# A state-space block's schedule: convolution one unit earlier, token products at the end of a job, inverse deviation left in PSUM, hinted loop edge

## The reference

```python
def _mamba_block(x, in_w, conv_w, conv_b, A_log, xd_w, xB_w, xC_w, dtp_w, dtp_b, D, out_w, g, b):
    xn = _layer_norm(x, g, b)
    xs, z = jnp.split(xn @ in_w, 2, axis=-1)
    xc = silu(causal_depthwise_conv4(xs) + conv_b)
    delta = softplus(xc @ xd_w @ dtp_w + dtp_b)
    Bm, Cm = xc @ xB_w, xc @ xC_w
    dA = exp(delta[..., None] * A)
    dBx = (delta * xc)[..., None] * Bm[:, :, None, :]
    y = _ssm_scan(dA, dBx, Cm) + D * xc       # h = dA * h + dBx; y = sum over 16 states of h * C
    return y * silu(z) @ out_w + x
fwd = blk(blk(x, 0), 1)
bwd = blk(blk(x[:, ::-1], 2), 3)[:, ::-1]
return jnp.concatenate([fwd, bwd], axis=-1) @ merge_w
```

## Time and profile before

| | |
|---|---|
| median of 3 runs | 10373.58 us (10369.56 to 10376.43) |
| the profiled execution's own time | 10389.18 us |
| its span, first to last instruction | 10387.4 us |
| busy, share of the span | PE 80%, PEld 66%, DVE 78%, POOL 68%, ACT 57% |
| Mamba phase, first scan to last | 144.1 to 8662.4 us |
| granted TensorE clock, mean over the span | 0.87 |

### The profile page before, as it was taken

How to read it: one execution, slowest core, us unless ns; L and a number is a source line. 1 busy time by engine, 2 the same in 40 slices (tenths; PEclk the granted TensorE clock), 3 DMA queues, 4 the chain that set the end, 5 groups by cost and what they waited for, 6 DMA issues and landing times. The chain is left out here.

```text
span 10387.4 us, 152898 instructions
## 1 busy us (share of the span) xinstructions
PE 8344.1 (80%) x42776; PEld 6881.5 (66%) x42776; DVE 8087.7 (78%) x10482; ACT 5899.2 (57%) x9202; POOL 7059.5 (68%) x7227
## 2 busy tenths in 40 slices
PE   5877777777878787878787877787877776999998
PEld 4666666666666666666666666676666664777776
DVE  4888889888988888888898888888888894333332
ACT  4565656565665666566566666665566662444443
POOL 4888888888888888888888888888888883000000
PEclk8888888888888888888888888888888887999998
DMA  2222222222222222222222222222222220000000
GB/s 93 94 89 99 92 98 91 99 92 93 92 94 93 90 98 93 90 79 90 89 98 93 98 91 97 93 98 92 90 93 96 92 90 25 11 10 10 12 9 9
DMA packets 414916, 819.68 MB, mean 79 GB/s; under 512 B 148919, under 2 KB 194139, under 8 KB 414043
## 3 DMA queue, kind: packets, MB, share of 16 engines
q1 hardware_dynamic: 410328, 806.69, 22.3%
q10 hardware_dynamic: 3714, 2.89, 0.1%
HBM read 783.16 MB, written 26.30 MB: 78 GB/s over the span
## 5 line engine op out<-in xcount | busy, mean ns | idle before, releaser
L776 ACT ACTIVATE decay<-delta,neg_a 128x512 f32<-128x512 f32 x4096 | 2793.0, 688 | 2484.5 <-DVE h_ps L978 1112.7
L544 POOL TENSOR_TENSOR bu<-b_all,u_buf 128x512 f32<-128x512 f32 x3072 | 3579.4, 1191 | 151.6 <-DVE h_ps L978 148.3
L978 DVE TENSOR_TENSOR_SCAN h_ps<-decay,bu 128x512 f32<-128x512 f32 x2304 | 2782.6, 1222 | 454.6 <-ACT decay L776 376.3
L1233 PE MATMUL y_ps<-ident,ch 128*128 128x128 f32 x16384 | 2579.9, 309 | 637.4 <-DVE ch L998 362.7
L1233 PEld LDWEIGHTS y_ps<-ident,ch 128*128 128x128 f32 x16384 | 2226.7, 161 | 1016.2 <-DVE ch L998 484.4
L556 POOL TENSOR_TENSOR ch<-ch,c_all 128x512 f32<-128x512 f32 x1024 | 1325.5, 1294 | 1112.1 <-DVE ch L978 910.0
L998 DVE TENSOR_TENSOR ch<-h_ps,c_all 128x512 f32<-128x512 f32 x3072 | 1977.2, 671 | 0.0
L547 POOL TENSOR_TENSOR bu<-b_all,u_buf 128x514 f32<-128x514 f32 x1024 | 1245.6, 1237 | 66.8 <-issue 56.3
L1117 PE MATMUL w_ps<-xn,in_w 128*128 128x257 f32 x4096 | 1074.8, 408 | 170.5 <-ACT xn L665 83.6
L982 DVE TENSOR_TENSOR_SCAN h_ps<-decay,bu 128x256 f32<-128x256 f32 x1536 | 1046.7, 737 | 125.3 <-POOL bu L547 98.2
L1117 PEld LDWEIGHTS w_ps<-xn,in_w 128*128 128x128 f32 x4096 | 799.9, 206 | 320.2 <-issue 81.1
(11 more groups left out here) (258 smaller groups left out, 11583.9 us busy)
## 6 DMA issues: line engine op xcount, KB each, us to landing
b_all<-bc_dram SPq DMA_DIRECT2D x512, 514.0 KB, 8.6
c_all<-bc_dram SPq DMA_DIRECT2D x512, 514.0 KB, 10.0
in_w<-in_L_attn_in_w SPq DMA_DIRECT2D x64, 1024.0 KB, 5.0
diag_store<-diag_dram SPq DMA_DIRECT2D x256, 256.0 KB, 2.9
x_in<-in_x SPq DMA_DIRECT2D x128, 256.0 KB, 2.6
out_w<-in_L_attn_out_w SPq DMA_DIRECT2D x64, 512.0 KB, 3.9
skip_diag<-skip_dram SPq DMA_DIRECT2D x64, 256.0 KB, 4.1
h_mid<-h_cur SPq DMA_DIRECT2D x32, 257.0 KB, 2.2
```

Of the source, the lines that this page charges most:

```text
L544: pool.tensor_tensor(bu[:, s % NBU, 0:NB * L].rearrange("p (b t) -> p b t", b=NB), b_all[:, n // NU, n % NU, :, 1:], u_buf[:, c % 2, :, 1: ...
L776: func(decay[:, s % NDP, :].rearrange("p (b t) -> p b t", b=NB), delta[:, c, :, 1:S], ACT.Exp, scale=neg_a[:, k, c, n:n + 1]).then_inc(dec ...
L978: dve.tensor_tensor_scan(h, decay[:, s % NDP, :], bu[:, s % NBU, 0:NB * L], 0.0, ALU.mult, ALU.add).then_inc(scan_done, 1)
L1233: last = pe.matmul(y_ps[:, k, :], ch[:, s % NPR, k * P:(k + 1) * P], ident[:, :], is_transpose=True, start=False, stop=(n == NST - 1 and k ...
```

## The change

It moves rows of the hand-written schedule and changes one buffer:

- `CONV_AT` is 14 in place of 15: projection, convolution, Silu, `xp` and the early step sizes of the next job stand one unit earlier (the Silu in unit 23). `y_at` keeps 12 or 14 and 18 and has 26 in place of 25; as its list position moves too, `y1` stands behind both halves of convolution 1.
- ACT copies the third chunk's sums in unit 25, behind the Silu, in place of just ahead of it in unit 24.
- The token products of job 2 move from units 10 to 13 to units 26 to 29, ACT's copies of them from units 12 and 14 to 28 and 30. The first two `x_in` loads go ahead of everything in job 2; the other six stand in `bring_bc`, two behind each of the pairs 1, 2 and 3 of `b_all` and `c_all`.
- The inverse deviation of a job is computed in place in PSUM (ACT's Ln and Exp), and DVE's two multiplications of the layer norm read it there; `rstd` in SBUF is left to the tokens and the step sizes. In jobs 1 to 3 DVE normalizes within unit 13, not behind it, and ACT applies gain and bias in unit 13, not 14. In job 4 `norm_at` is 10 in place of 11.
- The loop is opened with `hint_back_edge=True`: a row BRANCH_PREFETCH_HINT at the head of every round, on every engine.

```diff
@@ -25,7 +25,7 @@
 BLOCK_OF_JOB = (0, 2, 1, 3)
-CONV_AT = 15
+CONV_AT = 14
 EPS = 1e-5
@@ -49,8 +49,7 @@
-        first = norm[:2] + ["t0"] + norm[2:] + ["t1"] if tokens else norm
-        steps = first + conv + ["xp", "dt0", "dt1", "dt2", "dt3"]
+        steps = norm + conv + ["xp", "dt0", "dt1"] + (["t0", "t1"] if tokens else []) + ["dt2", "dt3"]
         return [(name, 4 if name in ("t0", "t1") else jj) for name in steps]
@@ -66,10 +65,8 @@
-        for name, before in [("y2", "xp"), ("y1", "cv1")] + [("y0", "t1"), ("y0", "xs0")]:
+        for name, before in [("y2", "dt1"), ("y1", "xs2"), ("y0", "xs0")]:
             at = [i for i, key in enumerate(keys) if key[0] == before]
-            if name == "y0" and ((name, jj) in keys or before == "t1" and not at):
-                continue
             keys = keys[:at[0]] + [(name, jj)] + keys[at[0]:] if at else [(name, jj)] + keys
@@ -102,14 +99,14 @@
     def y_at(jj):
-        return (14 if jj == 4 else 12), CONV_AT + 3, CONV_AT + 10
+        return (14 if jj == 4 else 12), 18, 26
...
     def norm_at(jj):
-        return 11 if jj == 4 else 9
+        return 10 if jj == 4 else 9
@@ -314,7 +311,7 @@
             period(0, 0, True, False)
-            with eng.Fori(0, GROUPS - 1) as g:
+            with nc.Fori(0, GROUPS - 1, engines=[eng.engine], hint_back_edge=True) as g:
                 for jj in (1, 2, 3, 4):
@@ -388,10 +385,12 @@
                                      ).then_inc(bc_loaded[n], 16)
-
-            def load_x(g, jj):
-
-                for n in range(8):
+                    if jj == 3 and not is_final(g) and n in (1, 2, 3):
+                        load_x(g, 4, (2 * n, 2 * n + 1))
+
+            def load_x(g, jj, part=range(8)):
+
+                for n in part:
                     c, b, half = n // 4, n // 2 % 2, n % 2
@@ -433,6 +432,8 @@
+                if jj == 2 and not is_final(g):
+                    load_x(g, 4, range(2))
                 if not first:
@@ -443,8 +444,6 @@
                     load_weights(jj + 1)
-                    if jj == 2 and not is_final(g):
-                        load_x(g, 4)
                     load_skip(g, jj + 1)
@@ -653,6 +652,12 @@
                 w = banks(name, g, jj)
+                if kind == "job":
+
+                    func(w[:, :, 0:S], w[:, :, 0:S], ACT.Ln, bias=eps_t[:, 0:1]).then_inc(rstd_logs, 1)
+                    act.wait_ge(rstd_logs, job_count(g, jj, 1, 1))
+                    func(w[:, :, 0:S], w[:, :, 0:S], ACT.Exp, scale=-0.5).then_inc(rstd_ready, 1)
+                    return
                 func(rstd[:, :, :], w[:, :, 0:S], ACT.Ln, bias=eps_t[:, 0:1]).then_inc(read_of(name, g, jj), 1)
@@ -660,7 +665,7 @@
                 k = BLOCK_OF_JOB[jj % 4]
-                act.wait_ge(xhat_ready, job_count(g, jj, 1, 1))
+                act.wait_ge(read_of("var", g, jj), nth("var", g, jj))
                 for c in range(CM):
@@ -846,11 +851,11 @@
                     centred(g, jj + 1, 1)
-                if jj == 2 and not is_final(g) and u == 12:
-                    tokens(g, 4, 0)
+                if jj == 2 and not is_final(g) and u in (28, 30):
+                    tokens(g, 4, (u - 28) // 2)
                 if u == norm_at(jj) + 3:
                     inverse_deviation("job", g, jj + 1)
-                if u == norm_at(jj) + (4 if jj == 4 else 5):
+                if jj == 4 and u == norm_at(jj) + 4:
                     gain_and_bias(g, jj + 1)
@@ -885,8 +890,8 @@
                     centred(g, jj + 1, 0)
-                if jj == 2 and not is_final(g) and u == 14:
-                    tokens(g, 4, 1)
+                if jj != 4 and u == norm_at(jj) + 4:
+                    gain_and_bias(g, jj + 1)
                 if u == CONV_AT + 1:
@@ -908,12 +913,10 @@
                     lead(g, jj, NU * u + NDP, last)
-                    if u % PAIRS == 1 and u // PAIRS != 3 and not (first and u == 1):
+                    if u % PAIRS == 1 and not (first and u == 1):
                         token_rows(g, jj - (u == 1), (u // PAIRS - 1) % CI)
...
                     lead(g, jj, NU * u + NDP + 1, last)
-                    if u == silu_at(jj)[1]:
-                        token_rows(g, jj, u // PAIRS - 1)
                     after_odd(g, jj, u, first, last)
@@ -940,9 +943,10 @@
                 dst = x_f if kind == "tok" else cen
+                inverse = rstd[:, :, :] if kind == "tok" else banks("var", g, jj)[:, :, 0:S]
                 for c in range(CM):
-                    last = dve.tensor_tensor(dst[:, c, :, :], cen[:, c, :, :], rstd[:, :, :], ALU.mult)
-                last.then_inc(x0_ready if kind == "tok" else xhat_ready, 1)
+                    last = dve.tensor_tensor(dst[:, c, :, :], cen[:, c, :, :], inverse, ALU.mult)
+                last.then_inc(x0_ready if kind == "tok" else read_of("var", g, jj), 1)
@@ -1056,6 +1060,8 @@
                         output(g, jj, y_at(jj).index(u - 1))
+                    if jj != 4 and not last and u == norm_at(jj) + 4:
+                        normalize("job", g, jj + 1)
                     if jj == 4 and u in (6, 8):
@@ -1084,7 +1090,7 @@
                         normalize("tok", g, 4)
-                    if u == norm_at(jj) + (3 if jj == 4 else 4):
+                    if jj == 4 and u == norm_at(jj) + 3:
                         normalize("job", g, jj + 1)
@@ -1298,8 +1304,6 @@
                         centre(g, jj + 1, [u - norm_at(jj)])
-                    if jj == 2 and not is_final(g) and 10 <= u < 14:
-                        tokens(g, 4, (u - 10) // 2, (u - 10) % 2)
                     if u == norm_at(jj) + 2:
@@ -1321,6 +1325,8 @@
                         step_input(g, jj + 1, steps.index(u))
+                    if jj == 2 and not is_final(g) and 26 <= u < 30:
+                        tokens(g, 4, (u - 26) // 2, (u - 26) % 2)
```

More of the change, by code:

```diff
@@ L248, in mamba_phase @@
         rstd_ready = sem("rstd_ready")
-        xhat_ready = sem("xhat_ready")
+        rstd_logs = sem("rstd_logs")
         xn_ready = sem("xn_ready")
```

## The result

The changed kernel takes 10205.8 us (median of four runs, 10198.6 to 10211.6), the kernel before 10375.0 in the same session: a ratio of 0.9836, 95% interval 0.9819 to 0.9853. That is 1.6% faster, some 170 us; 218 were forecast. The time lies inside the range of 10080 to 10290, and inside the likeliest case's own range. The profiled spans, 10387.4 and 10209.9 us, differ by 177.5.

The account below looks back on a forecast made before the run. DVE's list of waits was taken to decide; terms of -67, -126, +69, -36, -31, -15 and -12 sum to -218 us, giving 10171 for the profiled execution, 10156 us against the median. The range was 10080 to 10290.

Parts of the forecast that it names:

- likeliest case: Whole kernel: all terms near their size, 10156 us, own range 10080 to 10230; chance 55%.
- loop edge (unit 0 of job 1): Head of each round: the hint takes back 4.8 us at each of 14 edges, -67 us; bounds 0 and -72.
- behind the Silu (units 25 to 27): DVE's wait behind the convolution's Silu falls from 3.35 to 1.7 us, small waits partly; 2.0 x 63, -126 us.
- y1 (unit 19): Second chunk's sums come later behind both halves of convolution 1: +1.1 us a job, +69 us; bounds 0.5 and 1.8.
- step sizes (unit 30, `sp_l`): The step sizes' logarithm comes a unit sooner and covers DVE's 0.57 us wait in each job: -36 us.
- layer norm's products, busy: DVE's 128 multiplications shorten from 975 to about 690 ns with one operand in PSUM: -31 us; bounds 0 and -37.
- job 4 (its units 12 to 18): Earlier norm removes part of DVE's 2.0 us wait, lengthens the Silu's stall by 1.3: net -15 us; bounds 0 and -30.
- token products (job 2, units 13, 29, 31): Moving them frees 7.8 us a round and costs 7 in units 26 to 30: -12 us.
- the hint does nothing: Rival at the loop edge: the late start stays despite the hint, 10223 us; chance 15%.
- both rivals that made the term longer: Token products: halved PE clock or 6 us landings, +105 us, 10261, 13%; images landing like the broadcasts, +267, 10423, 7%.

Follow-up runs that it names:

- Experiment 3: Kernel before with only ACT's copy of the third chunk's sums moved behind the Silu (unit 25) and y2 turned back one unit later: 10700.4 us, 1.0313.
- Experiments 11 and 12: Changed kernel with y1 turned back in unit 19: 10214.4 us; the same plus ACT's copy of convolution 1 half a unit later: 10161.9 us.
- experiment 4: Changed kernel with the jobs' inverse deviation back in SBUF (`rstd`): 10250.6 us, 0.9882.
- Experiment 5: Changed kernel with job 4's centred copies behind the first and second decay after the gates' Silu: 10220.8 us, 0.9856.
- Experiments 6 to 9: Changed kernel, job 2: three of four token products out, 10168.1 us; six image loads out, 10148.5; token products partly later, 10200.2; last half in job 3, 10227.7.

## Why the prediction was right, point by point

I added up DVE's idle time by unit over jobs 1 to 62 of both traces (waits of more than 0.15 us), and its busy time. Idle fell from 932.5 to 792.5 us, busy by 33.2 in the whole span; the sum, 173, is near the 177.5 of the spans.

| term | forecast | measured |
|---|---|---|
| loop edge (unit 0 of job 1) | -67 | -70 |
| behind the Silu (units 25 to 27) | -126 | -104 |
| y1 (unit 19) | +69 | +49 |
| step sizes (unit 30, `sp_l`) | -36 | -36 |
| layer norm's products, busy | -31 | -37 |
| job 4 (its units 12 to 18) | -15 | +32 |
| token products (job 2, units 13, 29, 31) | -12 | +20 |

What the table leaves out, some 30 us less idle time, is small pieces: units 12 and 17 of job 2 (14), unit 20 (9), unit 13 of jobs 1 and 3 (9).

So the mechanisms were right, and the total was helped by luck. The terms of the table come to 146 us where the forecast had 218. Of the 72 that are missing, the small pieces, which nobody had priced, gave some 30 back. One thing isn't separated by any run: the mean granted clock rose from 0.870 to 0.886 and PE's busy time fell by 55 us. How much of the waits on PE went by that, and not by the order of the lists, is not shown.

**Loop edge: right in size, incomplete in its cause.** All 5 us of the edge went, where 4.8 were taken. The rival "the hint does nothing" is out: alone it brings 80 us. But the prediction gave the hint the whole 67, and in the changed kernel it carries 40 to 45 of them. The rule of the Trainium skill (Runtime: NRT & Kernel Launch, Instruction fetch mechanics), that prefetch is purely sequential and a taken branch forces a fetch, taken to the letter was that rival, and the runs with the hint go against it: 54 packets of q14 fewer, and no wait at the edge. Whether the prefetch is sequential without the hint no run here shows.

**The Silu: right in its mechanism, mis-sized by a sixth.** The main wait is 1.7 us in three jobs of four, as worked out, and 2.1 in the other. The two small waits, 0.3 each, were to "go in part" (one of them stands ahead of the stall, not behind it); in their place a wait is left in unit 27, 0.5 in the mean. The prediction had booked the sums' copy in unit 25 at nothing, because ACT has time there. Experiment 3 shows what that rests on: PE waits for this copy's bank, and the copy costs nothing only because the Silu and `xp` moved up with it. I had not named that cover.

**y1: right.** 0.8 us a job more, between the bounds of 0.5 and 1.8, where 1.1 was taken. Experiments 11 and 12 add that y1 isn't the cause. Convolution 1 is late, and ACT's copy of it would have been the next to stall.

**Step sizes and layer norm: right**, the second at its bound of -37. Its 31 came of taking 128 x 0.69 = 88 from a busy time of 119.9, in which records that overlap count once. Counted alike on both sides it is 119.9 to 82.5, or 128 x 0.29, both 37. And the reason is not what the nearest row suggested, a shorter read: the products no longer wait for POOL (experiment 4).

**Job 4: the step that failed, in sign.** "Removes part of the 2.0 us" was true, the 25 us of that wait went down to 11. But the Silu's stall, unit 13's waits for decays, doubled, from 37 to 76 us (2.6 a round more, where 1.3 was taken), and decays and `bu` in units 14 to 18 added some 6. The rows of ACT and DVE in unit 13 of the round shown:

```profile
2288.67 0.60 ACT L645 ACTIVATE sq<-w_ps 128x514 f32<-128x514 f32 x1 [1.59 <-PE w_ps L1123]
...
2287.20 1.23 DVE L982 TENSOR_TENSOR_SCAN h_ps<-decay,bu 128x512 f32<-128x512 f32 x1 [3.58 <-ACT decay L781]
...
2290.46 1.23 DVE L982 TENSOR_TENSOR_SCAN h_ps<-decay,bu 128x512 f32<-128x512 f32 x1 [2.03 <-ACT decay L781]
```

DVE's two waits were 2.61 and 0.70 us in the kernel before. The copy right behind the Silu is two operations of ACT, 1.1 us, and makes the first wait 1.0 longer. The next copy waits 1.59 us for PE, as it did before, but there two decays were out ahead of the first copy and now none is, so DVE pays 1.3 of it. The prediction had priced the first and not the second. Experiment 5 found no gain in the later place, so this looks like the price of an earlier norm, not of a bad order within it.

**The token products: right in their mechanism, mis-sized by 2 us a round.** Starts, steps and the end of the first copy came within a microsecond. The term was short by the two ACT operations between copy and decay, 1.3 us, and t1 was full at 30.8 in place of 29.8. Lost are 8.8 a round (7 forecast), freed 7.5 (7.8). The landing, 2.5 to 4.2 us in that round, lies around the lower end of what was taken (3.5 to 5), and the granted clock from the first pair to the end of job 2 is 0.85 in the mean, not half. So both rivals that made the term longer are out. Experiments 6 to 9 say why none of the places tried was free: a start that PE's list allows only at 8.9 us, four pairs of some 4 us of PE and their images form one chain, which ends some 30 us after unit 25 begins, and whoever stands behind its end pays, be it a decay in unit 29, a decay in job 3, or y3.

## What to carry to other kernels

Before a copy out of PSUM is moved to a later place, look at who writes that bank next: here it cost 5 us a job through PE, though the copy itself took its 0.6 us as before. When a wait disappears and another of the same size comes up on another engine, look for what both wait for: here it was a late convolution, and moving one consumer gained nothing, moving both 40 us. And price a part of a change both alone and as the last one in, since the two can differ by half: the hint was worth 80 us alone and 40 to 45 as the last part. And before a shorter mean is put down to where an operand lies, look at its spread: here all of the difference was waiting for another engine.

## What the runs showed of the hardware

A product on DVE with both operands in SBUF (`cen` by `rstd`, 128x514 f32) takes 680 to 695 ns when POOL runs nothing beside it and up to 1751 when it does, 967 to 975 in the mean; the long ones of the kernel before end 542 to 556 ns after the POOL instruction that was under way at their start. With one operand in PSUM it takes 681 to 693 ns, whatever POOL does.

The loop edge without a hint costs DVE 2.9 to 5.2 us, through POOL's late start, and some four 8 KB packets and two 16 KB packets of code more per edge.

An image of 256 KB lands in 2.5 to 5.3 us between the bursts (median 3.4 over the trace of the changed kernel), and in 2.4 to 4.6, median 2.8, with none between the images.
